# Pair 0's opening in a per-sample convolution: new group statistics, a residual put into copied weights, and another order of the first products

## The reference

```python
xn = group_norm(x, groups=32)                  # two channels a group, biased variance, eps 1e-5
pooled = xn.mean(axis=(2, 3))                  # 32 x 64
a = relu(pooled @ fc1_w.T + fc1_b)             # K = 4 hidden units
att = softmax(a @ fc2_w.T + fc2_b, axis=1)     # 32 x 4
agg_w = einsum('bk,koihw->boihw', att, weight) # a 64x64x3x3 kernel of its own for each image
agg_b = att @ bias
out = x + conv3x3(xn, agg_w, pad=1) + agg_b
```

## Time and profile before

| | us |
|---|---|
| median of 3 runs | 309.03 (308.75 to 310.32) |
| the profiled execution | 308.6 |
| its span | 306.8 |
| PE busy in the span | 298.9 (97%) |
| VectorE busy | 244.3 (80%) |
| ScalarE busy | 187.1 (61%) |
| GpSimd busy | 23.4 (8%) |
| granted TensorE clock, mean | 0.999 |

### The profile page before, as it was taken

The page is one execution under the profiler, slowest core; times in us unless marked ns, Lnnn a source line. Parts: engine busy times, 40 slices in busy tenths (PEclk is TensorE's granted clock), DMA queues, the critical chain, the costliest instruction groups (busy, mean ns, idle before and its releaser), DMA issues.

```text
span 306.8 us, 15852 instructions
## 1 busy us (share of the span) xinstructions
PE 298.9 (97%) x7068; PEld 263.5 (86%) x7068; DVE 244.3 (80%) x764; ACT 187.1 (61%) x242; POOL 23.4 (8%) x36
## 2 busy tenths in 40 slices
PE   8789999999999999999999999999999999999995
PEld 6557998789987997789977777799999999999884
DVE  3998897979999998888898989878696978856000
ACT  1292929467292938558296868677784866768222
POOL 1005040220500000000000000000000000000000
PEclk9999999999999999999999999999999999999999
DMA  6892864947577575848646767595757352332333
GB/s 206 309 417 95 230 169 130 261 104 224 165 216 182 148 223 129 242 139 220 179 134 163 240 174 252 160 252 148 220 136 216 101 148 64 109 94 77 100 114 102
DMA packets 31444, 53.62 MB, mean 175 GB/s; under 512 B 6800, under 2 KB 24080, under 8 KB 31376
## 3 DMA queue, kind: packets, MB, share of 16 engines
q1 hardware_dynamic: 31152, 52.52, 58.5%
q10 hardware_dynamic: 224, 0.09, 0.1%
HBM read 26.89 MB, written 25.69 MB: 171 GB/s over the span
## 4 chain that ended last, share of the span: by engine, by line
PE 93%; DVE 2%; DMA 2%; ACT 1%; issue 1%; SPq 0%; DVEq 0%
PE acc L855 92%; DMA x<-x 2%; DVE stats L345 1%; ACT xh L670 1%; DVE wparts L364 0%; PE tiny L823 0%; SPq L263 0%; ACT wh L708 0%; ACT mix L714 0%; DVE o L635 0%; DVE mv L353 0%; DVE newton L394 0%; DVE sums L408 0%; DVE logit L428 0%; DVE rstd L396 0%
## 5 line engine op out<-in xcount | busy, mean ns | idle before, releaser
L855 PE MATMUL acc<-xh,wh 64*64 64x385 f16 (+5 forms) x2304 | 111.8, 325 | 0.9 <-ACT wh L708 0.9
L855 PE MATMUL acc<-xh,wl 64*64 64x385 f16 (+5 forms) x2304 | 111.4, 325 | 0.0
L855 PE MATMUL acc<-xl,wh 64*64 64x385 f16 (+5 forms) x2304 | 111.2, 325 | 0.0
L855 PEld LDWEIGHTS acc<-xh,wh 64*64 64x64 f16 x2304 | 86.3, 107 | 12.2 <-ACT wh L708 1.6
L855 PEld LDWEIGHTS acc<-xh,wl 64*64 64x64 f16 x2304 | 87.8, 107 | 10.0
L855 PEld LDWEIGHTS acc<-xl,wh 64*64 64x64 f16 x2304 | 88.0, 107 | 9.6
L734 ACT ACTIVATE o<-acc,par 128x392 f32<-128x392 f32 (+1 forms) x64 | 42.8, 669 | 55.2 <-PE acc L855 55.2
L345 DVE BATCH_NORM_STATS2 stats<-x 128x6 f32<-128x448 f32 x112 | 65.1, 615 | 4.5 <-DMA x<-x 4.5
L682 ACT ACTIVATE xh<-x,xof,xsc 128x1568 f16<-128x1568 f32 x24 | 40.5, 1690 | 31.3 <-DVE xof L419 31.3
L543 DVE TENSOR_TENSOR xl<-x,xh 128x1568 f16<-128x1568 f32 x28 | 49.8, 1783 | 7.7 <-ACT x L645 7.6
L460 DVE SCALAR_TENSOR_TENSOR mix<-w_sb,ex,mix 128x192 f32<-128x192 f32 (+1 forms) x72 | 44.0, 611 | 0.5
(11 more groups left out here) (64 smaller groups left out, 143.3 us busy)
## 6 DMA issues: line engine op xcount, KB each, us to landing
x<-x SPq DMA_DIRECT2D x48, 392.0 KB, 4.3
out<-o SPq DMA_DIRECT2D x61, 196.0 KB, 3.8
out<-o SPq DMA_DIRECT2D x122, 98.0 KB, 2.9
x<-x SPq DMA_DIRECT2D x6, 784.0 KB, 9.6
x<-x SPq DMA_DIRECT2D x7, 224.0 KB, 5.0
w_sb<-w_t SPq DMA_DIRECT2D x2, 288.0 KB, 3.1
w_sb<-w_t SPq DMA_DIRECT2D x1, 576.0 KB, 5.4
crossed<-par SPq DMA_DIRECT2D x32, 0.5 KB, 2.5
```

The lines of the kernel that those rows point to most:

```text
L855: ins = nc.tensor.matmul(pixels[:, top:bottom, left:right], weights[i][halves[m], tap * C:(tap + 1) * C], window, start=start and step == ...
```

## The change

The input of pair 0 comes in five DMAs instead of seven; the weights wait for the third of them, and the later inputs for weight set 1 instead of set 0. In `group_stats`, for every pair, the statistics of both channels of a group are brought together ahead of one aggregate, eps is put into one of the raw statistics, and the power on GpSimd gives way to a first guess from the bits of the variance and two refining steps on VectorE. For pair 0 the bound on the weights is a norm, from squares on ScalarE and one root on GpSimd. The middle row of the four weight sets is copied by ScalarE (`wmiddle`), VectorE adds the diagonal to all four copies ahead of the mixture, and the addition behind the mixture goes. ScalarE's order of `high_strip` changes; TensorE's order in pair 0 becomes, for each row of taps, xh wh of three groups and then xh wl of the same; `wl` is made in three parts. From pair 4 on, `logits` comes ahead of a chunk of statistics that it stood behind. The core of the diff:

```diff
+PIECES = ((0, 1), (1, 2), (2, 4), (4, 6), (6, 7))
+PIECE_OF = (0, 1, 2, 2, 3, 3, 4)
+GATE = 2
+ROOT_BITS = float(0x5F3759DF)
+DOWN = 2.0 ** -40
-WARM_PRODUCTS = (54, 10, 10, 6, 6, 4)
+WARM_PRODUCTS = (46, 10, 10, 6, 6, 4)
-SUMS_AT = ((1, 2, 3), (1, 2, 2), (1, 2, 2), (1, 2, 2), (1, 0, 8), ...
+SUMS_AT = ((1, 2, 6), (1, 2, 2), (1, 2, 2), (1, 1, 8), (1, 0, 8), ...
...
 (sync)
-            for n in range(CHUNKS):
-                pixels = slice(n * CHUNK, (n + 1) * CHUNK)
-                sp.dma_start(x_sb[0][:, pixels], x_d[0, :, pixels]).then_inc(x_chunk[n], 16)
-            sp.wait_ge(x_chunk[4], 16)
+            for n, (first, end) in enumerate(PIECES):
+                pixels = slice(first * CHUNK, end * CHUNK)
+                sp.dma_start(x_sb[0][:, pixels], x_d[0, :, pixels]).then_inc(x_piece[n], 16)
+            sp.wait_ge(x_piece[GATE], 16)
...
-            sp.wait_ge(s_weights[0], 16)
+            sp.wait_ge(s_weights[1], 16)
...
 (gpsimd)
-            def take_root(p):
-                pool.wait_ge(s_var, p + 1)
-                nc.gpsimd.tensor_tensor(root[:], var[:], minus_half[:], ALU.pow).then_inc(s_root, 1)
+            pool.wait_ge(s_wsquares, 2)
+            nc.gpsimd.tensor_tensor(wnorms[:], wsquares[:], half_power[:], ALU.pow).then_inc(s_wnorms, 1)
+            for p in range(EARLY):
+                second_low_inputs(p)
...
 (vector)
+            def swap_stats(p, first, end):
+                columns = slice(6 * first, 6 * end)
+                return nc.vector.stream_shuffle(stats[:, 1, columns], stats[:, 0, columns], swap)
 (chunk_stats)
+                    if p >= 1 and t == 0:
+                        dve.wait_ge(s_norm, p)
+                    if p == 0 and t == CHUNKS - 1:
+                        dve.wait_ge(s_most, 1)
+                        dve.wait_ge(s_eps, 1)
+                        swap_stats(0, 0, CHUNKS - 1).then_inc(s_other, 1)
...
+                    elif t == 2:
+                        dve.wait_ge(s_chunk, p + 1)
+                        nc.vector.tensor_scalar(stats[:, 0, 2:3], stats[:, 0, 2:3], EPS * PIX, None,
+                                                ALU.add).then_inc(s_eps, 1)
...
 (group_stats: the shuffle of the means, its sums of means and variances, the root and
  the three steps behind it go, and largest_weights and first_range of VectorE too)
+                nc.vector.bn_aggr(own[:], stats[:, 0, :]).then_inc(gch, 1)
+                dve.wait_ge(s_other, p + 2)
+                glink(n + 2, nc.vector.bn_aggr(mv[:], stats[:].rearrange("p a b -> p (a b)")))
+                var = mv[:, 1:2]
+                ts(guess[:].bitcast(mybir.dt.int32), var.bitcast(mybir.dt.int32), -0.5, ROOT_BITS, ALU.mult,
+                   ALU.add).then_inc(gch, 1)
+                ts(vhalf[:], var, -0.5, None, ALU.mult)
+                tt(diff[:], own[:, 0:1], mv[:, 0:1], ALU.subtract).then_inc(gch, 1)
+                dve.wait_ge(gch, n + 4)
+                stt(out=square[:], in0=guess[:], scalar=guess[:], in1=var, op0=ALU.mult, op1=ALU.mult).then_inc(gch, 1)
+                ts(part_guess[:], guess[:], 0.375, None, ALU.mult)
...
+                stt(out=series[:], in0=square[:], scalar=-10.0 / 3.0, in1=square[:], op0=ALU.add,
+                    op1=ALU.mult).then_inc(gch, 1)
...
+                stt(out=better[:], in0=series[:], scalar=5.0, in1=part_guess[:], op0=ALU.add,
+                    op1=ALU.mult).then_inc(gch, 1)
...
+                ts(fdiff[:], small_sb[:, FC1:FC1 + K], diff[:], None, ALU.mult)
...
+                glink(n + 8, stt(out=newton[:], in0=better[:], scalar=better[:], in1=vhalf[:], op0=ALU.mult, op1=ALU.mult))
+                stt(out=rstd[:], in0=newton[:], scalar=1.5, in1=better[:], op0=ALU.add, op1=ALU.mult).then_inc(s_rstd, 1)
+                dve.wait_ge(s_rstd, p + 1)
...
+                if 1 <= p < PAIRS - 1:
+                    chunk_stats(p + 1, 0, 1)
...
+            def first_mixture():
+                dve.wait_ge(s_exp, 1)
+                dve.wait_ge(s_diagonal, 1)
+                dve.wait_ge(s_middle, 2)
+                for k in range(K):
+                    share(0, k, PARTS[0], k, (s_part, s_part, s_part, s_mix)[k])
+                    scale_step(0, k)
+                for n, part in enumerate(PARTS[1:], 1):
+                    if n == 2:
+                        dve.wait_ge(s_share, 1)
+                    for k in range(n - 1, K):
+                        share(0, k, part, shares(0, n) + k - (n - 1))
+                        if k == n:
+                            low_part(n - 1)
+                        if n == 1:
+                            params_step(0, k)
+                normalise_first_quarter()
+                low_part(2)
+            def residual_in_weights():
+                for n in range(3):
+                    dve.wait_ge(s_weights[n], 16)
+                dve.wait_ge(s_std, 1)
+                nc.vector.scalar_tensor_tensor(
+                    out=wmiddle[:, :, C:2 * C], in0=eye[:].unsqueeze(1).to_broadcast([P, K, C]), scalar=std[0][:],
+                    in1=w_sb[:, :, CENTRE * C:(CENTRE + 1) * C], op0=ALU.mult, op1=ALU.add).then_inc(s_diagonal, 1)
+            def low_part(n):
+                dve.wait_ge(s_wh, n + 1)
+                part = PARTS[n]
+                nc.vector.scalar_tensor_tensor(out=wl[0][:, part], in0=mix[:, part], scalar=wsc[0][:], in1=wh[0][:, part],
+                                               op0=ALU.mult, op1=ALU.subtract).then_inc(s_wl, 1)
...
-            largest_weights(1)
             logits(0)
-            largest_weights(2)
-            first_range()
-            mixture_in_parts(0)
-            normalise_first_quarter()
-            low_weights(0)
+            residual_in_weights()
+            first_mixture()
             weights_bound()
+            chunk_stats(1, 0, 1)
             dve.wait_ge(s_scaled, 1)
             low_inputs(0, 0)
-            chunk_stats(1)
+            chunk_stats(1, 1, CHUNKS)
...
 (scalar)
+            def squares(k):
+                act.wait_ge(s_weights[k], 16)
+                if k >= 1:
+                    act.wait_ge(s_wsquares, k)
+                nc.scalar.activation(mix[:], w_sb[:, k, :], ACT.Square, scale=DOWN,
+                                     accum_out=wsquares[:, k:k + 1]).then_inc(s_wsquares, 1)
+            def copy_middle(first, end):
+                act.wait_ge(s_weights[2 if end == K else 1], 16)
+                row, copied = (t[:, first:end, columns].rearrange("p k (t c) -> p k t c", c=C)[:, :, 0:3:2]
+                               for t, columns in ((w_sb, PARTS[0]), (wmiddle, slice(0, 3 * C))))
+                nc.scalar.activation(copied, row, ACT.Copy).then_inc(s_middle, 1)
...
+            for k in range(2):
+                squares(k)
+                copy_middle(2 * k, 2 * k + 2)
             high_strip(1)
             exponentials(0)
-            high_strip(4)
-            first_share(1)
-            high_strip(2)
-            high_strip(5)
-            high_strip(3)
+            for n in (4, 2, 5):
+                high_strip(n)
             high_weights_part(0, 0)
+            for n in (3, 6):
+                high_strip(n)
             first_share(2)
-            high_strip(6)
             high_strip(0)
             high_weights_part(0, 1)
             high_strip(7)
+            normalise_quarter(0, 1)
             high_weights_part(0, 2)
...
 (tensor)
-                pe.wait_ge(s_wpart, 1)
-                nc.tensor.matmul(tiny[0][:, WEIGHTS:WEIGHTS + 1], scale[:], wpart[:],
+                pe.wait_ge(s_wnorms, 1)
+                for k in range(2):
+                    ins = nc.tensor.matmul(tiny[1][:, WEIGHTS:WEIGHTS + 1], scale[:], wnorms[:, k:k + 1],
+                                           start=k == 0, stop=k == 1)
...
+            for n in range(len(PARTS)):
+                steps = range(3 * n, 3 * n + 3)
+                pe.wait_ge(s_wh, n + 1)
+                for g in range(SLOTS):
+                    if (n, g) == (0, 0):
+                        pe.wait_ge(s_strip, 2)
...
+                    high(0, g, steps)
+                pe.wait_ge(s_wl, n + 1)
+                for g in range(SLOTS):
+                    products(0, g, wl, xh, steps)
```

More of the change, by code:

```diff
@@ L121, in dynamic_conv @@
         eye = sb("eye", [P, C])
[L122 removed]
+        half_power = sb("half_power", [P, 2])
         b1_part = sb("b1_part", [P, K])
         warm = sb("warm", [P, 1])
[L125 removed]
+        wsquares = sb("wsquares", [P, 2])
+        wnorms = sb("wnorms", [P, 2])
         wbound = sb("wbound", [P, 1])
[L127 to L129 removed]
+        stats = sb("stats", [P, 2, CHUNKS * 6])
+        own = sb("own", [P, 2])
         mv = sb("mv", [P, 2])
[L131 to L138 removed]
+        guess = sb("guess", [P, 1])
+        vhalf = sb("vhalf", [P, 1])
+        square = sb("square", [P, 1])
+        part_guess = sb("part_guess", [P, 1])
+        series = sb("series", [P, 1])
+        diff = sb("diff", [P, 1])
+        newton = sb("newton", [P, 1])
```

(26 more changed lines are left out.)

170 lines of the change are left out of this document (78 added, 92 removed).

## The result

The changed kernel takes 309.90 us (median of 12 runs, 307.53 to 311.38) against 308.57 for the kernel before (12 runs). The ratio is 1.0039, 95% interval 1.0024 to 1.0055: slower by 0.4%, where a small gain was forecast. The profiled execution took 310.86, its span is 309.1. The runs spread over 3.9 us and sort themselves by TensorE's granted clock, averaged over each run: the two at 1.000 took 307.53 and 308.28, the two at 0.994 308.69 and 309.09, the eight at 0.989 309.56 to 311.38.

The account below looks back on a forecast made before the run. TensorE, busy 97% of the span, was taken as the bound, leaving only the opening: first product at 16.8 instead of 17.32 gains 0.5, stalls give back 0.2, so 308.4 us; overall range 307.1 to 309.9.

Parts of the forecast that it names:

- the fall: Rival: TensorE's clock drops in two gaps before the convolution, halving its products' pace for some 4 us: 310.2; chance 0.05.
- Its price: Clock rival's cost: convolution begins at the low clock for some 4 us, losing half of that, 2 us: 310.2.
- Statistics' end: Pair 0's input in larger pieces: VectorE's statistics end at 10.3 instead of 9.44, 0.85 later (0.3 to 1.3).
- The chain: Group statistics, from end of statistics to the last sum: 2.6 us (2.4 to 2.8), 0.75 less than before.
- Diagonal and mixture: Diagonal ahead of pair 0's mixture: a 0.5 us instruction costs 0.1 in front; 0.35 goes behind the mixture.
- Weights: ScalarE's last copy waits for weight sets 2 and 3, landing between 12.8 and 13.4; TensorE's start taken as 16.8.
- a rival from 13.9 on: Sets 2 and 3 landing late, at 14.3 or later, delay exponentials and TensorE's start to 17.9: 309.6; chance 0.09.
- Behind the start: TensorE's stalls after its first product: 0.6 against 0.42 before, 0.2 worse (-0.2 to +0.7).
- Strip 6: After the first 24 products TensorE waits for this strip, which ends 1.66 after the high weights' start: 0.2 lost.
- Pairs 2 to 15 kept their 17.76 us: TensorE is busy for all 17.76 us of a pair behind the opening; lighter VectorE or GpSimd can't shorten that.

Follow-up runs that it names:

- e1: Changed kernel with 60 and 20 warm products in the first two groups instead of 46 and 10, filling both gaps: 308.36 us, ratio 0.9997 to the kernel before.
- e4: Kernel before with 38 warm products at first instead of 54, opening a gap ahead of the end of statistics: 308.83 us, ratio 1.0019.
- e2: Changed kernel with 60 warm products at first instead of 46, filling only the first gap: 308.13 us, ratio 0.9983 to the kernel before.
- e3: Changed kernel with 20 products in the second warm group instead of 10, filling only the second gap: 308.86 us, ratio 1.0005 to the kernel before.
- e9: Changed kernel with seven input pieces and weights behind the third chunk, keeping its own 46 warm products: 307.31 us, ratio 0.9973 to the kernel before.
- e11: Changed kernel with its last four groups of warm products cut from 10, 6, 6, 4 to 2 each: 309.91 us, ratio 1.0045 to the kernel before.
- e10: Kernel before with its weights waiting for the third input chunk instead of the fifth, nothing else: 308.32 us, ratio 1.0001.
- e6: Changed kernel with 60 warm products at first, seven input pieces, weights behind the third chunk: 306.80 us, ratio 0.9943 to the kernel before.
- e5: Changed kernel with 60 warm products at first, seven input pieces, weights behind the fifth chunk: 308.12 us, ratio 0.9987 to the kernel before.

## Why the prediction was wrong, step by step

**The step that failed** is in the rivals: "Each gap is no longer than the one that was harmless", by which the fall got a chance of 0.05. Each gap was indeed shorter than the 2.0 us of the earlier trace rows (1.68 and 1.32 in the trace), and the clock fell in 10 of 12 runs. Two things were wrong in it. The gaps stand in the prediction with nearly the right times, but were compared one by one, where they are a pair with ten products between; the kernel before had only 0.27 us ahead of its ten. And the harmless 2.0 us was one execution: the same kernel was below 0.996 in 9 of the 35 runs beside e1 to e4. e1, e2 and e4 show from both sides that the gaps ahead of the first product are the cause; how much each counts stays open (e3, e9, e11).

**Its price** was also read from the wrong place. I took half of the convolution's products at the low clock, 2 us, which gave 310.2; that the measured 309.9 is near it is luck. In the profiled run the convolution ran at it for only 0.2 us; what cost was the queue of warm products in front of the range and the first product, 2.7 us against e1 (this execution, at 310.86, is 1.0 above the median). e11 shows that both readings come to the same total if the low clock lasts long enough.

**Statistics' end:** 10.3 forecast, 10.62 measured. The third piece landed at 7.5 (range given: 6.5 to 7.5), and in the other traces with five pieces between 7.0 and 8.2, against 5.6 to 6.5 with seven. The cost of the larger pieces was seen, but mis-sized: 0.85 was forecast against the 9.44 of the kernel before, which was late itself (8.86 in e4, 8.85 in e10). Statistics end at 10.1 to 11.4 in the six traces with five pieces (middle 10.66) and at 8.9 to 9.5 in the five of the changed kernel with seven (middle 9.40): 1.3.

**The chain:** 2.6 forecast from there to the last sum, 2.59 measured (10.62 to 13.21). The wide aggregate took 0.475 (0.55 taken), the own one 0.33.

**Diagonal and mixture:** 0.48 for the instruction (0.5 forecast), 0.3 gained between exponentials and high weights (0.35 less 0.1 forecast).

**Weights:** ScalarE's last copy started at 13.29 in the changed kernel, where it held nothing up (the exponentials follow the logits' maximum by 0.03), and at 13.77 in e1 (12.8 to 13.4 taken), where they follow it by 0.46. This term is why e1 starts at 17.24 and not at the forecast 16.8, and e6 against e5, where only the gate differs, is its proof. It was seen as a rival from 13.9 on. From the copy's start to the exponentials are 0.93 in e1, so with the logits at the forecast 13.95 it costs something from some 13.0 on, and sooner where the statistics are earlier.

**Behind the start:** 0.2 worse forecast, 0.2 to 0.3 better measured. In e1 the sums of pair 1 were ready at 30.25 and their products came at 30.50, so nothing waited, and the low inputs didn't stop TensorE either. Strip 6 did: the first 36 products and the start of the next are 1.80 apart in e1 against 1.50 for the 36 behind them, 0.3 lost where 0.2 was forecast. Pairs 2 to 15 kept their 17.76 us, as said.

**From the end of statistics to the first product,** with the clock held, are 6.6 us in e1, e2 and e3 and 6.4 in e6; 6.5 was forecast (10.3 to 16.8), and the kernel before takes 7.9 (9.44 to 17.32, and the same in e10). So the new chain and order are worth 1.3 us of the 1.4 that were forecast, and by the estimate above the larger pieces take nearly all of it back.

So with the clock held the change is worth about what was forecast (0.1 and 0.5 us by the ratios of e1 and e2, with intervals that include nothing). In part that is luck: e1 starts 0.4 later than forecast and is 0.4 better behind its start. The granted clock takes the gain and 1.2 us more.

## What to carry to other kernels

Warm products that bridge a chain of small steps must be counted against the end of the step they bridge, not against the number that used to do; whoever makes the step later, or starts it at another time, has to count anew, with some to spare, since the same count ended anywhere between 8.0 and 9.2 us here, and check the clock over a dozen runs, since a single run at full clock proves little. When two inputs of a stage arrive together, sooner on one side shows nothing until the other is moved too: seven pieces alone brought nothing and early weights alone nothing in the old kernel, and together with the new chain they brought 1.7 us. A piece of input twice as large delays its first consumer (the third landed at 7.0 to 8.2 instead of 5.6 to 6.5), and fewer issues didn't pay for that here, where issuing wasn't the limit.

## What the runs showed of the hardware

With gaps of TensorE of 1.7 and 1.3 us (in the trace) and 1.3 us of products between them the clock fell in 10 of 12 runs, and in e11's trace it fell behind a single gap of 2.7. With gaps of 0.3 and 2.1 the kernel before had it below 0.996 in 9 of 35 runs beside e1 to e4. By the rule in the Trainium skill, TensorE: Matmul & The Clock Gate (Part 1: The HAM clock gate), the granted clock has only two values while one or two cores are busy, and the windows agree: 0.50 or 1.00, and others only where it changes. The low state lasted from 3.4 us (e4) to some 10 (e11). The record isn't the whole truth: in the first microseconds it says 1.00 while the warm products run at half pace, with 7 of them between 5 and 6 us where 12 are counted at full pace.

A Square beside exponentials needed no table load: the changed kernel has the one of 1.28 us at its start and no other.
